# Low parts of the attention values: subtracted by VectorE straight from the bank instead of by GpSimd from a copy

## The chip, the cores and the metric

One core of one Trainium2 chip. The metric is the device time of one execution in microseconds; the times are medians over several executions. Lower is better.

## What is computed

One layer of graph attention with a residual and a layer norm, over 128 graphs of 128 nodes with 512 features, 16 heads of 32, all in float32. The bias is twice the adjacency, since it is given for both encodings.

```python
q, k, v = (split_heads(x @ W.T) for W in (Wq, Wk, Wv))
a = jnp.einsum('bhnd,bhmd->bhnm', q, k) * D ** (-0.5) + (adj + adj)[:, None]
a = jnp.where(jnp.any(a != 0, axis=-1, keepdims=True), a, -jnp.inf)
p = jax.nn.softmax(a, axis=-1)
o = jnp.einsum('bhnm,bhmd->bhnd', p, v).transpose(0, 2, 1, 3).reshape(B, N, D)
return _layernorm(x + o @ Wo.T, axis=-1)
```

## The kernel before

**Precision.** Every product with a weight is split: an operand is a high part (float32 rounded to the form that TensorE takes in one pass, tiles `..._hi`) and a low part (the rest, `..._lo`). `split_product` (L543) makes three matmuls per piece, low x high, high x low, high x high, so 12 matmuls of 512 columns per product. The high part is a copy by ScalarE (ACT), `copy` at L753; the low part is a subtraction, whole minus high: `rest`, on GpSimd at L423 and on VectorE (DVE) at L919.

**Work.** Four graphs form a group (32 groups), four heads a tile (4 tiles per group). One tile of one group is a phase, f = 0 to 127. A phase on each engine:

- TensorE (L699): `scores(f)`, 64 small matmuls into the banks `ps_s`; then, in odd phases from 3 on, `values` of the two phases f-3 and f-2, each into a bank of its own; then four products by a fixed table (`PLAN`, L40): k and q of the next tile, one v, one output product o.
- DVE (L1081): `bias(f)`, 16 instructions of neg_a = -(scores + bias) with the row's minimum, `smallest` (a reduction over all of neg_a), `reciprocals`, `largest`, `stats` and `means` for the layer norm of a graph, `row_factors`, `normalise` and `turn_blocks` (32x32 transposes) for images 0 and 1, then the last four again for images 2 and 3.
- ACT (L876): `exps(f, i)` for images 0 to 3, each four exponentials that wait for that image's bias; after image 0 and after image 1, in odd phases, `values_hi` of the two values; between them `take`, the copies of products out of their banks; `chunk_hi`, the high parts of the inputs; and `normalise`, a row of the layer norm.
- GpSimd (L526): `add` (residual), `chunk_lo` (low parts of the inputs), `values_lo`, `ln` (nine tiny steps of a layer norm). It waits and works in exactly this order.
- SyncE: the DMAs. The transposed blocks leave through `save_blocks` (L336) for a buffer in HBM and come back turned through `move_blocks` (L346) into `e_t`, from which `values` reads. `values(f)` therefore comes two or three phases after the blocks of f.

**Values.** What `values` leaves in its bank is the input of the output products, and so it too has to be split. ACT makes `o_hi` from the bank, then, when GpSimd's subtraction before is over, a second, whole copy `o_sb` from the same bank; GpSimd subtracts `o_hi` from `o_sb` into `o_lo`. These are the lines of ACT (L846 to L851):

```python
copy(o_hi[:, o_slot(g, t), :], values_bank(f)[:, :]).then_inc(o_hi_done, 1)
if f < LAST - 1:
    if f:
        act.wait_ge(o_lo_done, f)
    act.wait_ge(o_hi_done, f + 1)
    copy(o_sb[:, :], values_bank(f)[:, :]).then_inc(values_copied, 1)
```

The four banks `ps_w` are handed round in the order of use (`bank_uses`, L90; `wait_bank`, L561): who wants one waits until its last user's content has been copied, for values until `values_copied`. The values of the last two phases are split by DVE already (`values_lo`, L932, and `values_lo_half`, L938).

Of the kernel before, what the change touches and what calls it, by code (L numbers as in the profile page):

```python
# [11 lines left out]
P = 128  # L12
# [6 lines left out]
TILES = CH  # L19
# [36 lines left out]
LAST = PHASES - 1  # L56
# [26 lines left out]
def valued(f):  # L83

    if f >= LAST - 1:
        return [f - 2]
    return [f - 3, f - 2] if f % 2 and f > 2 else []
# [13 lines left out]
def o_slot(g, tile):  # L101
    return tile + 2 * (g % PAIR) if tile < 2 else tile + 2
# [22 lines left out]
def build(nc, xt_d, x_d, adj_d, wq_d, wk_d, wv_d, wo_d, out_d, blocks_d):  # L125
    ctx = ExitStack()
    with ctx:
        def sb(name, shape, dt=F32):
            return ctx.enter_context(nc.sbuf_tensor(name, shape, dt))
# [4 lines left out]
        def sem(name):  # L134
            return ctx.enter_context(nc.semaphore(name))
# [13 lines left out]
        e_b = sb("e_b", [P, GG * TH * NODES])  # L149
        e_t = sb("e_t", [P, PAIR, GG * TH * NODES])  # L150
        y_sb = sb("y_sb", [P, 512])
        o_sb = sb("o_sb", [P, 512])
        o_hi = sb("o_hi", [P, TILES + 2, 512], F32R)
        o_lo = sb("o_lo", [P, TILES + 2, 512], F32R)
        ident = sb("ident", [P, P])
# [55 lines left out]
        v_copied = sem("v_copied")  # L211
        q_copied = sem("q_copied")
        k_copied = sem("k_copied")
# [16 lines left out]
        r_done = sem("r_done")  # L230
        normalised = sem("normalised")
        o_copied = sem("o_copied")
        values_copied = sem("values_copied")
        opened = sem("opened")
        preloaded = sem("preloaded")
        last_ve_done = sem("last_ve_done")
# [3 lines left out]
        last_lo_done = sem("last_lo_done")  # L240
        o_hi_done = sem("o_hi_done")
        o_lo_done = sem("o_lo_done")
# [26 lines left out]
        def values_bank(f):  # L269
            return ps_w[USE["values", f, 0] % BANKS]  # L270
# [138 lines left out]
        def _(pool):  # L409
# [13 lines left out]
            def rest(out, whole, hi):  # L423
                return pool.tensor_tensor(out, whole, hi.bitcast(F32), ALU.subtract)  # L424
# [7 lines left out]
            def add(f, s):  # L432

                todo = slots(f)
                if todo[s][0] == "o":
                    _, g, i = todo[s]
                    row = x_row(g, i)
                    if GG * g + i >= AHEAD_O:
                        pool.wait_ge(ahead_loaded, 16 * (LATE_O - AHEAD_O))
                    else:  # L440
                        pool.wait_ge(x_loaded[i], 16 * (g + 1))
                    pool.wait_ge(o_copied, count("o", g, i))
                    pool.tensor_tensor(row, y_sb[:, :], row, ALU.add).then_inc(added, 1)  # L443

            def values_lo(f):
                pool.wait_ge(values_copied, f + 1)
                rest(o_lo[:, o_slot(f // TILES, f % TILES), :], o_sb[:, :], o_hi[:, o_slot(f // TILES, f % TILES), :]
                     ).then_inc(o_lo_done, 1)

            def ln(f):  # L450

                n, i = f - O_LAG, (f - O_LAG - 1) % GG
                if n < 1:
                    return
                ve, minus_mean, y, vy, vyy, half, left = (ln_tmp[:, c:c + 1] for c in range(7))

                def own(c):
                    pool.wait_ge(pool_step, 8 * (n - 1) + c)

                if n > 1:  # L460
                    pool.wait_ge(rstd_done, n - 1)
                pool.wait_ge(mean_done, n)
                pool.tensor_tensor(ve, mean_var[:, i, 1:2], eps, ALU.add).then_inc(pool_step, 1)  # L463
                pool.tensor_tensor(minus_mean, mean_var[:, i, 0:1], minus_one, ALU.mult).then_inc(pool_step, 1)
                own(1)
                pool.tensor_tensor(y, ve, minus_half, ALU.pow).then_inc(pool_step, 1)
                own(3)
                pool.tensor_tensor(vy, ve, y, ALU.mult).then_inc(pool_step, 1)
                own(4)
                pool.tensor_tensor(vyy, vy, y, ALU.mult).then_inc(pool_step, 1)  # L470
                own(5)
                pool.tensor_tensor(half, vyy, minus_half, ALU.mult).then_inc(pool_step, 1)
                own(6)
                pool.tensor_tensor(left, half, one_and_half, ALU.add).then_inc(pool_step, 1)
                own(7)
                pool.tensor_tensor(rstd[:, i:i + 1], y, left, ALU.mult).then_inc(pool_step, 1)
                own(8)
                pool.tensor_tensor(shift[:, i:i + 1], minus_mean, rstd[:, i:i + 1], ALU.mult).then_inc(rstd_done, 1)
# [47 lines left out]
            for f in range(PHASES):  # L526
                if f:
                    add(f - 1, -1)
                chunk_lo(window_chunk(f))
                for p in valued(f):  # L530
                    values_lo(p)
                ln(f)
                chunk_lo(late_chunk(f))
                for s in range(len(slots(f)) - 1):
                    add(f, s)
# [6 lines left out]
        def _(pe):  # L542
# [18 lines left out]
            def wait_bank(u):  # L561

                if u >= BANKS:
                    kind, g, index = USES[u - BANKS]
                    free = {"k": k_copied, "q": q_copied, "v": v_copied, "o": o_copied, "values": values_copied}[kind]
                    n = g + 1 if kind == "values" else count(kind, g, index)
                    pe.wait_ge(free, n)

# [183 lines left out]
        def _(act):  # L752
            def copy(out, in_, scale=1.0):  # L753
                return act.activation(out, in_, ACT.Copy, scale=scale)  # L754
# [84 lines left out]
            def values_hi(f):  # L839
                g, t = f // TILES, f % TILES  # L840
                if t > 1 and g:
                    act.wait_ge(made["o"], GG * g)
                elif g > 1:
                    act.wait_ge(made["o"], GG * (g - 1))
                act.wait_ge(values_done, f + 1)
                copy(o_hi[:, o_slot(g, t), :], values_bank(f)[:, :]).then_inc(o_hi_done, 1)  # L846
                if f < LAST - 1:
                    if f:
                        act.wait_ge(o_lo_done, f)
                    act.wait_ge(o_hi_done, f + 1)  # L850
                    copy(o_sb[:, :], values_bank(f)[:, :]).then_inc(values_copied, 1)  # L851

            def values_hi_half(half):
                cols = slice(2 * P * half, 2 * P * (half + 1))
# [63 lines left out]
        def _(dve):  # L918
            def rest(out, whole, hi):  # L919
                return dve.tensor_tensor(out, whole, hi.bitcast(F32), ALU.subtract)  # L920
# [11 lines left out]
            def values_lo(f):  # L932

                slot = o_slot(f // TILES, f % TILES)
                dve.wait_ge(o_hi_done, f + 1)
                rest(o_lo[:, slot, :], values_bank(f)[:, :], o_hi[:, slot, :]).then_inc(last_lo_done, 1)

            def values_lo_half(half):  # L938
                cols = slice(2 * P * half, 2 * P * (half + 1))
# [59 lines left out]
            def bias(f):  # L999
                g = f // TILES  # L1000
                dve.wait_ge(scores_done, f + 1)
                dve.wait_ge(adj_done, g + 1)
                if f:
                    dve.wait_ge(exp_done, GG * f)
                    dve.wait_ge(abs_done, f)
                for i in range(GG):
                    for h in range(TH):
                        last = dve.tensor_tensor_reduce(  # L1008
                            out=neg_a[:, i, h, :], in0=ps_s[h][:, i * NODES:(i + 1) * NODES],
                            in1=adj_sb[:, g % PAIR, i, :], scale=-1.0, scalar=INF, op0=ALU.add, op1=ALU.min,  # L1010
                            accum_out=neg_max[:, i, h:h + 1])
                    last.then_inc(biased, 1)

            def smallest(f):
                dve.wait_ge(biased, GG * (f + 1))
                dve.tensor_reduce(neg_min[:, :].rearrange("p a b -> p (a b)"),  # L1016
                                  neg_a[:, :].rearrange("p a b c -> p (a b) c"), AX.X, ALU.max).then_inc(min_done, 1)
# [62 lines left out]
            dve.wait_ge(xt0_lo_done, CH)  # L1080
            for f in range(PHASES):  # L1081
                bias(f)
                smallest(f)
                reciprocals(f, 0)
                largest(f)
                if f < LAST:
                    stats(f - O_LAG - 1)
                any_nonzero(f)
                if f < LAST:
                    means(f - O_LAG - 1)  # L1090
                row_factors(f, 0)
                if f % TILES == TILES - 1 and f < LAST:
                    double_adj(f // TILES + 1)
                normalise(f, 0)
                if f < LAST:
                    turn_blocks(f, 0)
                else:
                    stats(f - O_LAG - 1)
                    means(f - O_LAG - 1)
                reciprocals(f, 1)  # L1100
                row_factors(f, 1)
                normalise(f, 1)
                if f < LAST:
                    turn_blocks(f, 1)
# [47 lines left out]
```

## Time and profile before

| | us |
|---|---|
| median of 3 runs (lowest to highest) | 1718.62 (1718.35 to 1719.05) |
| the profiled execution's own time | 1717.99 |
| its span, first to last instruction | 1716.2 |
| TensorE busy | 1698.0 (99%) |
| DVE busy | 1633.8 (95%) |
| ACT busy | 1368.4 (80%) |
| GpSimd busy | 962.2 (56%) |
| TensorE's granted clock, mean | 0.999 |

Busy time is the union of an engine's instructions. Matmuls overlap, so that a busy TensorE need not be at its peak. An instruction's duration on DVE and ACT is longer than the distance to the next one where both follow without a wait; the text says "gives way after" for that distance.

### The profile page before, as it was taken

Reading aid. Unit: us, or ns where it says so; the run is one execution under the profiler, and the core shown is the slowest. Engines: PE = TensorE matmul, PEld = TensorE weight load, DVE = VectorE, ACT = ScalarE, POOL = GpSimd, SP = SyncE. Lnnn points to the kernel's source line nnn. Section 1 sums busy time; section 2 is a strip of 40 time slices with the busy share of each in tenths; the row PEclk is TensorE's granted clock in tenths of the full one; section 3 lists DMA queues with packets and bytes.
Section 4 is the critical chain, followed back from the end, with each engine's and each line's share of the span. In section 5 each row is a group of like instructions: output and inputs, shape, how many; then the busy total and the mean of one; then the engine's idle time right before and its main releaser. Section 6 shows DMA issues by size and latency. Waiting matters only on the chain. (4 is left out here: it accounts for less than half of the span.)

```text
span 1716.2 us, 45980 instructions
## 1 busy us (share of the span) xinstructions
PE 1698.0 (99%) x14385; PEld 1383.8 (81%) x14385; DVE 1633.8 (95%) x5814; ACT 1368.4 (80%) x5135; POOL 962.2 (56%) x1512
## 2 busy tenths in 40 slices
PE   8999999999999999999999999999999999999998
PEld 7778888888888888888888888888888888888876
DVE  7999999999999999999999999999999999999997
ACT  7788788778877887788778878887888788778876
POOL 2346556565565565555655655556556556565554
PEclk9999999999999999999999999999999999999999
DMA  7677777777877777777777787777877777777775
GB/s 224 192 203 232 226 227 236 218 215 235 234 221 225 215 232 226 222 224 237 218 226 224 222 236 214 230 233 223 230 213 228 230 220 231 231 217 231 225 227 164
DMA packets 278068, 382.61 MB, mean 223 GB/s; under 512 B 25152, under 2 KB 159552, under 8 KB 277696
## 3 DMA queue, kind: packets, MB, share of 16 engines
q1 hardware_dynamic: 276768, 379.16, 75.3%
q8 instruction: 113, 1.85, 0.5%
q14 instruction: 131, 1.07, 0.2%
q10 hardware_dynamic: 1056, 0.52, 0.1%
HBM read 212.86 MB, written 166.72 MB: 221 GB/s over the span
## 5 line engine op out<-in xcount | busy, mean ns | idle before, releaser
L828 ACT ACTIVATE e_sb<-neg_a,neg_max 128x128 f32<-128x128 f32 x2048 | 793.1, 391 | 185.5 <-DVE neg_max L1008 185.5
L1008 DVE CUSTOM_DVE_ANT_0 neg_a<-ps_s,adj_sb 128x128 f32<-128x128 f32 x2048 | 440.2, 285 | 11.0 <-PE ps_s L634 9.4
L555 PE MATMUL ps_w<-xt_hi,w_lo 128*128 128x512 f32 x1020 | 412.8, 405 | 0.0
L556 PE MATMUL ps_w<-xt_lo,w_hi 128*128 128x512 f32 x1020 | 399.6, 392 | 0.0
L828 ACT ACTIVATION_READ_ACCUMULATOR e_sb<-neg_a,neg_max 128x1 f32 x2048 | 388.9, 190 | 0.0
L1064 DVE STREAM_TRANSPOSE e_b<-e_sb 128x1024 f32<-128x1024 f32 x254 | 316.3, 1245 | 27.3 <-DVE e_sb L1054 0.9
L1054 DVE SCALAR_TENSOR_TENSOR e_sb<-e_sb,r_inv 128x1024 f32<-128x1024 f32 x256 | 318.5, 1244 | 7.9 <-DVE r_inv L1048 0.2
L1016 DVE TENSOR_REDUCE neg_min<-neg_a 128x16 f32<-128x2048 f32 x128 | 292.7, 2286 | 4.4
L424 POOL TENSOR_TENSOR o_lo<-o_sb,o_hi 128x512 fp32r<-128x512 f32 x126 | 163.5, 1298 | 213.8 <-ACT o_sb L754 213.8
L558 PE MATMUL ps_w<-xt_hi,w_hi 128*128 128x512 f32 x1020 | 273.3, 390 | 0.0
L555 PEld LDWEIGHTS ps_w<-xt_hi,w_lo 128*128 128x128 f32 x1020 | 191.5, 188 | 57.5 <-issue 12.7
L558 PEld LDWEIGHTS ps_w<-xt_hi,w_hi 128*128 128x128 f32 x1020 | 191.6, 188 | 40.9
L463 POOL TENSOR_TENSOR ln_tmp<-mean_var,constants 128x1 f32<-128x1 f32 x122 | 31.8, 261 | 343.3 <-DVE mean_var L971 343.3
L556 PEld LDWEIGHTS ps_w<-xt_lo,w_hi 128*128 128x128 f32 x1020 | 191.7, 188 | 37.0
L556 PE MATMUL ps_w<-w_lo,xt_hi 128*128 128x512 f32 x512 | 199.3, 389 | 0.0
L443 POOL TENSOR_TENSOR x_sb<-y_sb,x_sb 128x512 f32<-128x512 f32 x121 | 155.3, 1283 | 78.5 <-ACT y_sb L754 78.5
L555 PE MATMUL ps_w<-w_hi,xt_lo 128*128 128x512 f32 x512 | 199.2, 389 | 0.0
L555 PE MATMUL ps_w<-w_hi,o_lo 128*128 128x512 f32 x496 | 193.2, 390 | 1.7 <-POOL o_lo L424 1.7
L556 PE MATMUL ps_w<-w_lo,o_hi 128*128 128x512 f32 x496 | 193.1, 389 | 0.0
L754 ACT ACTIVATE y_sb<-ps_w 128x512 f32<-128x512 f32 x124 | 74.0, 597 | 129.9 <-PE ps_w L558 129.7
L1008 DVE DVE_READ_ACCUMULATOR2_ANT neg_max<- 128x1 f32 x2048 | 170.8, 83 | 0.0
L634 PEld LDWEIGHTS ps_s<-k_sb,q_sb 32*128 32x128 f32 x4096 | 126.0, 186 | 49.6 <-issue 49.6
(125 smaller groups left out, 2795.7 us busy)
## 6 DMA issues: line engine op xcount, KB each, us to landing
blocks<-e_b SPq DMA_DIRECT2D x1016, 128.0 KB, 2.2
e_t<-blocks SPq DMA_DIRECT2D x126, 1024.0 KB, 7.3
x_sb<-x SPq DMA_DIRECT2D x121, 256.0 KB, 4.9
out<-x_sb SPq DMA_DIRECT2D x121, 256.0 KB, 3.4
xt_raw<-xt SPq DMA_DIRECT2D x120, 256.0 KB, 4.9
adj_sb<-adj SPq DMA_DIRECT2D x32, 256.0 KB, 5.2
neg_a<-xt SPq DMA_DIRECT2D x4, 256.0 KB, 5.7
v_sb<-wv SPq DMA_DIRECT2D x4, 256.0 KB, 7.7
```

What stands on the lines that cost most here:

```text
L424: return pool.tensor_tensor(out, whole, hi.bitcast(F32), ALU.subtract)
L443: pool.tensor_tensor(row, y_sb[:, :], row, ALU.add).then_inc(added, 1)
L555: pe.matmul(out, lhs_lo(c), rhs_hi(c), start=(c == 0), stop=False)
L556: pe.matmul(out, lhs_hi(c), rhs_lo(c), start=False, stop=False)
L558: last = pe.matmul(out, lhs_hi(c), rhs_hi(c), start=False, stop=(c == chunks - 1))
L634: last = pe.matmul(ps_s[h][:, nodes], q_sb[rows, slot, nodes], k_sb[rows, slot, nodes], start=True, stop=True)
L754: return act.activation(out, in_, ACT.Copy, scale=scale)
L828: last = act.activation(e_sb[:, i, h, :], neg_a[:, i, h, :], ACT.Exp, scale=-1.0, bias=neg_max[:, i, h:h + 1], accum_out=sums[:, i, h:h + 1])
L1008: last = dve.tensor_tensor_reduce(out=neg_a[:, i, h, :], in0=ps_s[h][:, i * NODES:(i + 1) * NODES], in1=adj_sb[:, g % PAIR, i, :], scale=- ...
L1016: dve.tensor_reduce(neg_min[:, :].rearrange("p a b -> p (a b)"), neg_a[:, :].rearrange("p a b c -> p (a b) c"), AX.X, ALU.max).then_inc(mi ...
L1054: dve.scalar_tensor_tensor(out=e_sb[:, two].rearrange("p i h n -> p (i h) n"), in0=e_sb[:, two].rearrange("p i h n -> p (i h) n"), scalar=BIG,
L1064: dve.transpose(blocks[:, half], e_sb[:, 2 * half:2 * half + 2].rearrange("p i h (b j) -> p (i h) b j", b=BLOCKS)).then_inc(transposed, 1)
```

## The change

In `values_hi` the second copy goes, with its two waits; `o_sb` and the semaphore `values_copied` go; GpSimd's `values_lo` goes. DVE runs its own `values_lo`, which subtracts `o_hi` from the bank itself, for every phase, between `bias(f)` and `smallest(f)`. The bank of a value is free when that subtraction is over (`o_lo_done`).

```diff
@@ gpsimd
-            def values_lo(f):
-                pool.wait_ge(values_copied, f + 1)
-                rest(o_lo[:, o_slot(f // TILES, f % TILES), :], o_sb[:, :], o_hi[:, o_slot(f // TILES, f % TILES), :]
-                     ).then_inc(o_lo_done, 1)
...
                 chunk_lo(window_chunk(f))
-                for p in valued(f):
-                    values_lo(p)
                 ln(f)
@@ tensor, wait_bank
-                    free = {"k": k_copied, "q": q_copied, "v": v_copied, "o": o_copied, "values": values_copied}[kind]
+                    free = {"k": k_copied, "q": q_copied, "v": v_copied, "o": o_copied, "values": o_lo_done}[kind]
@@ scalar, values_hi
                 copy(o_hi[:, o_slot(g, t), :], values_bank(f)[:, :]).then_inc(o_hi_done, 1)
-                if f < LAST - 1:
-                    if f:
-                        act.wait_ge(o_lo_done, f)
-                    act.wait_ge(o_hi_done, f + 1)
-                    copy(o_sb[:, :], values_bank(f)[:, :]).then_inc(values_copied, 1)
@@ vector, values_lo
                 dve.wait_ge(o_hi_done, f + 1)
-                rest(o_lo[:, slot, :], values_bank(f)[:, :], o_hi[:, slot, :]).then_inc(last_lo_done, 1)
+                rest(o_lo[:, slot, :], values_bank(f)[:, :], o_hi[:, slot, :]
+                     ).then_inc(o_lo_done if f < LAST - 1 else last_lo_done, 1)
@@ vector, the loop over phases
                 bias(f)
+                for p in valued(f):
+                    values_lo(p)
                 smallest(f)
```

DVE, odd phase 5, from the end of its bias on. `ISA ... 128x128` is a bias instruction, `neg_max 128x1` the row minimum that goes with it; after the change the line numbers are those of the changed kernel. Before:

```order
L1008 ISA neg_a,neg_max<-ps_s,adj_sb 128x128
L1008 ISA neg_max 128x1
L1016 TENSOR_REDUCE neg_min<-neg_a 128x16 [waits biased]
L1039 RECIPROCAL recip<-sums 128x8 [waits exp_done,r_done]
L1023 SCALAR_TENSOR_TENSOR abs_max<-neg_max,neg_min 128x16 [waits min_done,nonzero_done]
L1031 TENSOR_SCALAR nonzero<-abs_max 128x16 [waits abs_done,r_done]
L1048 SCALAR_TENSOR_TENSOR r_inv<-recip,nonzero 128x8 [waits nonzero_done,recip_done,normalised]
```


Now:

```order
L995 ISA neg_a,neg_max<-ps_s,adj_sb 128x128
L995 ISA neg_max 128x1
L906 TENSOR_TENSOR o_lo<-ps_w,o_hi 128x512 [waits o_hi_done] x2
L1003 TENSOR_REDUCE neg_min<-neg_a 128x16 [waits biased]
L1026 RECIPROCAL recip<-sums 128x8 [waits exp_done,r_done]
L1010 SCALAR_TENSOR_TENSOR abs_max<-neg_max,neg_min 128x16 [waits min_done,nonzero_done]
L1018 TENSOR_SCALAR nonzero<-abs_max 128x16 [waits abs_done,r_done]
L1035 SCALAR_TENSOR_TENSOR r_inv<-recip,nonzero 128x8 [waits nonzero_done,recip_done,normalised]
```


Two subtractions, each waiting for its high part, stand ahead of the minimum and of all that follows in the phase.

ACT, the odd phase from its first exponential on (`x3` is three more of the four). Before:

```order
L828 ACTIVATE e_sb,sums<-neg_a,neg_max 128x128 [waits biased,transposed]
L828 ACTIVATE e_sb,sums<-neg_a,neg_max 128x128 x3
L754 ACTIVATE o_hi<-ps_w 128x512 [waits values_done,o_made]
L754 ACTIVATE o_sb<-ps_w 128x512 [waits o_hi_done,o_lo_done]
L828 ACTIVATE e_sb,sums<-neg_a,neg_max 128x128 [waits biased]
L828 ACTIVATE e_sb,sums<-neg_a,neg_max 128x128 x3
L754 ACTIVATE o_hi<-ps_w 128x512 [waits values_done,o_made]
L754 ACTIVATE o_sb<-ps_w 128x512 [waits o_hi_done,o_lo_done]
L754 ACTIVATE k_sb<-ps_w 128x512 [waits k_made]
```


Now:

```order
L819 ACTIVATE e_sb,sums<-neg_a,neg_max 128x128 [waits biased,transposed]
L819 ACTIVATE e_sb,sums<-neg_a,neg_max 128x128 x3
L745 ACTIVATE o_hi<-ps_w 128x512 [waits values_done,o_made]
L819 ACTIVATE e_sb,sums<-neg_a,neg_max 128x128 [waits biased]
L819 ACTIVATE e_sb,sums<-neg_a,neg_max 128x128 x3
L745 ACTIVATE o_hi<-ps_w 128x512 [waits values_done,o_made]
L745 ACTIVATE k_sb<-ps_w 128x512 [waits k_made]
```


Between the two high parts only the exponentials of image 1 are left.

## Rows read from the trace of the kernel before

**Rows 1.** The page's first part: busy time and share of each engine.

```profile
PE 1698.0 (99%) x14385; PEld 1383.8 (81%) x14385; DVE 1633.8 (95%) x5814; ACT 1368.4 (80%) x5135; POOL 962.2 (56%) x1512
```

**Rows 2.** Who waited for whom, whole span: total us, times, longest.

```profile
DVE neg_a L1008 <- PE ps_s L634: 9.4, 26, 1.4
...
PE ps_w L658 <- DMA e_t<-blocks: 0.4, 1, 0.4
```

**Rows 3.** Timeline of TensorE, 800 to 831 us: start, duration, instruction.

```profile
804.47 1.17 PE L634 MATMUL ps_s<-k_sb,q_sb 32*128 32x128 f32 x32
...
817.78 1.95 PE L658 MATMUL ps_w<-e_t,v_sb 128*32 128x128 f32 x64
...
825.28 0.39 PE L555 MATMUL ps_w<-w_hi,xt_lo 128*128 128x512 f32 x1
...
830.81 0.39 PE L634 MATMUL ps_s<-k_sb,q_sb 32*128 32x128 f32 x4
```

**Rows 4.** Timeline of DVE, 805 to 833 us; idle time before it in brackets.

```profile
805.71 0.29 DVE L1008 CUSTOM_DVE_ANT_0 neg_a<-ps_s,adj_sb 128x128 f32<-128x128 f32 x1
...
812.61 0.17 DVE L1048 SCALAR_TENSOR_TENSOR r_inv<-recip,nonzero 128x8 f32<-128x8 f32 x1
812.81 1.23 DVE L1054 SCALAR_TENSOR_TENSOR e_sb<-e_sb,r_inv 128x1024 f32<-128x1024 f32 x1
...
817.11 1.25 DVE L1064 STREAM_TRANSPOSE e_b<-e_sb 128x1024 f32<-128x1024 f32 x1
818.28 0.25 DVE L1008 CUSTOM_DVE_ANT_0 neg_a<-ps_s,adj_sb 128x128 f32<-128x128 f32 x1
...
821.75 2.29 DVE L1016 TENSOR_REDUCE neg_min<-neg_a 128x16 f32<-128x2048 f32 x1
...
825.15 1.06 DVE L1048 SCALAR_TENSOR_TENSOR r_inv<-recip,nonzero 128x8 f32<-128x8 f32 x1
826.24 1.23 DVE L1054 SCALAR_TENSOR_TENSOR e_sb<-e_sb,r_inv 128x1024 f32<-128x1024 f32 x1
...
830.54 1.25 DVE L1064 STREAM_TRANSPOSE e_b<-e_sb 128x1024 f32<-128x1024 f32 x1
832.05 0.29 DVE L1008 CUSTOM_DVE_ANT_0 neg_a<-ps_s,adj_sb 128x128 f32<-128x128 f32 x1 [0.26 <-PE ps_s L634]
```

**Rows 5.** Timeline of DVE, the end of the next odd phase.

```profile
857.09 1.25 DVE L1064 STREAM_TRANSPOSE e_b<-e_sb 128x1024 f32<-128x1024 f32 x1
858.39 0.29 DVE L1008 CUSTOM_DVE_ANT_0 neg_a<-ps_s,adj_sb 128x128 f32<-128x128 f32 x1
```

**Rows 6.** Timeline of DVE, first bias of phase 3 and of phase 127.

```profile
55.35 0.25 DVE L1008 CUSTOM_DVE_ANT_0 neg_a<-ps_s,adj_sb 128x128 f32<-128x128 f32 x1
...
1689.76 0.29 DVE L1008 CUSTOM_DVE_ANT_0 neg_a<-ps_s,adj_sb 128x128 f32<-128x128 f32 x1 [1.07 <-PE ps_s L634]
```

**Rows 7.** Timeline of GpSimd, 814 to 828 us.

```profile
816.01 1.04 POOL L478 TENSOR_TENSOR shift<-ln_tmp,rstd 128x1 f32<-128x1 f32 x1
...
824.89 1.29 POOL L424 TENSOR_TENSOR o_lo<-o_sb,o_hi 128x512 fp32r<-128x512 f32 x1 [1.41 <-ACT o_sb L754]
```

**Rows 8.** Timeline of ACT, 819 to 826 us.

```profile
819.28 0.40 ACT L828 ACTIVATE e_sb<-neg_a,neg_max 128x128 f32<-128x128 f32 x1 [1.38 <-DVE neg_max L1008]
...
820.84 0.57 ACT L754 ACTIVATE o_hi<-ps_w 128x512 fp32r<-128x512 f32 x1
...
824.71 0.59 ACT L754 ACTIVATE k_sb<-ps_w 128x512 f32<-128x512 f32 x1
825.18 0.40 ACT L828 ACTIVATE e_sb<-neg_a,neg_max 128x128 f32<-128x128 f32 x1
```

**Rows 9.** Timeline of DVE, the two subtractions at the kernel's end.

```profile
1701.31 0.69 DVE L920 TENSOR_TENSOR o_lo<-ps_w,o_hi 128x512 fp32r<-128x512 f32 x1 [0.27 <-ACT o_hi L754]
1701.92 0.41 DVE L920 TENSOR_TENSOR o_lo<-ps_s,o_hi 128x256 fp32r<-128x256 f32 x1
```

**Rows 10.** Transfers into e_t issued between 834 and 900 us.

```profile
DMA to landing us min/median/max: 6.9/7.0/8.4
```

More of the change, by code:

```diff
@@ L151, in build @@
         y_sb = sb("y_sb", [P, 512])
-        o_sb = sb("o_sb", [P, 512])
         o_hi = sb("o_hi", [P, TILES + 2, 512], F32R)
@@ L232, in build @@
         o_copied = sem("o_copied")
-        values_copied = sem("values_copied")
         opened = sem("opened")
```

## The prediction

> **What bounds the kernel now.** I read the page's busy times first. TensorE is busy 99% of the span, VectorE (DVE) 95%, ScalarE (ACT) 80%, GpSimd (POOL) 56% [rows 1]. Two engines stand near full, so the next view is who waits for whom. DVE waits for scores only 26 times, 9.4 us in all, and TensorE waits for the transposed blocks once [rows 2]. Neither engine waits for the other to speak of: two chains have almost the same length.
>
> The timelines show which is longer. From scores to scores over two phases, TensorE takes 830.81 - 804.47 = 26.34 us [rows 3], and it has matmuls all the way. DVE's biases have the same distance, 832.05 - 805.71 = 26.34, and in it DVE stands still once: its last transpose starts at 830.54, such a transpose gives way to the next instruction after 1.17 us (817.11 to 818.28), so it could go on at 831.71, and it starts at 832.05, released by TensorE: 0.34 us free in this pair [rows 4]. In the next pair, which also doubles the adjacency, 857.09 + 1.17 = 858.26 against 858.39: 0.13 us free [rows 5]. **So TensorE sets the pace, with DVE 0.47 us in 52.68 behind it** (805.71 to 858.39, four phases). The whole loop confirms the group: from the bias of phase 3 to that of phase 127 it is 1689.76 - 55.35 = 1634.4 us [rows 6], 31 groups of 52.7.
>
> **The change, part by part.** Phases are numbered f = 0 to 127; in every odd f from 3 to 125 the values of two earlier phases are handled, 62 times.
>
> *GpSimd's 126 subtractions go.* They are on GpSimd, which has time. But one of them touches DVE. In an even phase the row factors at 812.61 give way to the next instruction after 0.20 us; in the odd phase the same instruction, at 825.15, lasts 1.06 and gives way after 1.09 [rows 4]. It ends at 826.21, and GpSimd's second subtraction, started at 824.89, ends at 826.18 [rows 7]: DVE was held until GpSimd had finished. With that subtraction gone I take back 0.89 us per odd phase. Bounds: 0, if something else of GpSimd's stands there then, and 1.09. I take 0.89, because in even phases, where GpSimd has only its small layer norm steps at this place, the row is short.
>
> *ACT's 126 second copies go.* ACT has time; what counts is that its second high part comes earlier. After the first exponential of an odd phase at 819.28, four of them take 1.56 us (to the first high part at 820.84), a copy gives way after 0.47 (824.71 to 825.18) and ends after 0.57 [rows 8]. Without the copy into o_sb the second high part ends at 819.28 + 1.56 + 0.47 + 1.56 + 0.57 = 823.44.
>
> *DVE gets 126 subtractions, two in a row between its bias and its minimum in odd phases.* The nearest row is the same subtraction, from the bank, at the kernel's end: 0.69 us long, and the next starts 0.61 after it [rows 9]. The first needs the high part that ended at 820.84 + 0.57 = 821.41, and starts at once when the bias is through, about 821.7. The second has to wait for the high part of 823.44; with a handover of some 0.06 it starts at 823.50, and the minimum follows at 824.11 where it started at 821.75 [rows 4]. **That is +2.36 us per odd phase: 1.22 of work and 1.14 of waiting for ACT.** Behind the waiting instruction stands all of DVE's phase: minimum, factors, both normalisations, both transposes and the next bias; ACT's exponentials of images 2 and 3 do not hang on it. Bounds: 1.22, if the high part came in time, and 2.6, if ACT starts a little late too. I take the timeline's 2.36.
>
> The Trainium skill, page "VectorE: DVE Perf Modes", section "The DRAIN you can't avoid", says that the next operation does not start until the pipeline has emptied. By that each subtraction would cost its full length, 0.69 where the rows show the next one 0.61 behind, and the sum would come out about 10 us higher; the trace decides, and I keep 0.61.
>
> *The bank is given back by DVE, not by ACT's copy.* The v and o products of the same phase, behind k and q, reuse these two banks. The first subtraction is over at about 822.4 and the second at 824.2, and the v product began at 825.28, the o product after it [rows 3]: no cost. The tile o_lo is complete at about 824.2 instead of 826.2, so the output products have it earlier. The buffer and two waits of ACT (for the old subtraction, and for its own first copy) go for nothing.
>
> *What is late next.* When DVE is the slower one, TensorE runs ahead until it meets the transposed blocks, which hang on DVE's transposes over two DMA hops. Their last hop lands 7.0 us after issue in the median, and TensorE waits for it only once in the profile [rows 2, 10]. So TensorE will stand at the values in odd phases by about what DVE lost, at most some 2 us. That costs nothing: values that start even 0.5 us after the bias has begun take 1.95 us [rows 3] and are done before ACT turns to the first high part, 2.6 us after that beginning (818.28 to 820.84). GpSimd's adding of the inputs comes earlier relative to DVE, but it stands behind the layer norm chain in GpSimd's own order, whose last step at 816.01 is held by DVE's second normalisation [rows 7]; so it cannot fall on that one.
>
> **The sum.** Four phases: 52.68, minus the free 0.34 and 0.13, minus 2 x 0.89, plus 2 x 2.36, is 55.15 us of DVE work without a gap, longer than TensorE's 52.68. That is +2.47 per group, times 31: +76.6. Phase 126 handles one value, +0.61 more. The last phase has another 0.61 ahead of its minimum, and there ACT's exponentials start earlier by the copy that is gone: I set it at nothing. Together +77 us. The profiled execution had a span of 1716.2 and took 1717.99, 0.6 below the median of the three runs; so 1718.6 + 77 = 1796 us. The three runs lie within 0.7 us, and about 0.2% (3.4 us) is what a measurement of this kernel can tell from no change.
>
> **Rivals.**
>
> *A: TensorE stays the bound, not slower.* The time freed on DVE (0.89 per odd phase and the 0.47 of gaps) pays for the subtractions. That decides the other way if 4 subtractions plus their waits cost no more than 52.68 - 50.43 = 2.25 us per group, 0.56 each with no wait. The rows speak against both: 0.61, and the second high part 1.1 us late. With slots of 0.61 and no wait it would be 50.43 + 2.44 = 52.87, +6 us, 1725; with slightly shorter slots 1718.6. For it: TensorE's higher busy share. Chance 0.05.
>
> The Trainium skill, page "Perfetto Trace Analysis", section "Identifying the Most-Contended Engine", takes the engine with the highest share as the one to optimise (and itself warns that matmul busy time misleads). By that rule TensorE stays the bound as long as DVE's busy time, 1634 + 77 - 55, is below 1698 [rows 1], and the time stays at 1718.6. It is this rival's case, and I give it no more than its 0.05, since an engine that works in order pays for its waits as well.
>
> *B: the held instruction stays held.* Something else of GpSimd's, an addition or a chunk subtraction shifted by the new lag, falls on a DVE instruction that it can hold. Price 0.89 per odd phase, 62 times: +55, 1851 us. For it: the 1.09 shows such holds are real. Against: in GpSimd's order nothing but the layer norm steps is left between the chunk's subtraction and the next addition. Chance 0.08.
>
> *C: the wait for the second high part is smaller or larger than I read*, by half: 62 x 0.57 = 35 us either way, 1761 or 1831. Against: every piece of that chain is a row. Chance 0.10.
>
> *D: TensorE loses speed when it stands still for a while*, or the blocks come so late that both engines wait in turn. One more us per pair would be 1858. Chance 0.03.
>
> **How the numbers follow.** The forecast has the remaining 0.74. Its own spread is 0.2 us per odd phase, 12 us, so 1784 to 1808; taking in part of C on both sides the range is 1776 to 1822. Faster needs something that no row shows: 0.01. Within 0.2% needs rival A with shorter slots: 0.03. Slower by over 0.2%: 0.96.
>
> **What would show it.** In the new profile DVE is busy about 1634 + 77 - 55 = 1656 us of 1793 and TensorE still 1698; DVE has some 62 waits of about 1.1 us at the subtraction, released by ACT's o_hi, about 70 us in all; 126 subtractions of 0.69; no wait of DVE for scores in the loop; the row factors near 0.17 us in odd phases too; pairs of phases at about 27.5 us, odd ones near 14.9 and even ones still 12.57; TensorE with idle time at the values or in front of them, some 1.2 us per pair. It would be wrong if the odd phase of DVE is not longer by about 1.5 us net, if the subtraction does not wait for ACT, or if DVE still waits for scores.

## The result, and the profile after

| | before | after |
|---|---|---|
| median, us | 1718.84 | 1794.97 |
| lowest to highest, us | 1718.35 to 1719.58 | 1793.28 to 1795.61 |
| ratio, 95% interval | | 1.0441 (1.0429 to 1.0454) |
| profiled execution, its span, us | 1716.2 | 1792.7 |
| DVE busy, us | 1633.8 | 1652.2 |
| TensorE busy, us | 1698.0 | 1713.5 |

The change makes the kernel 76 us slower. Forecast were 77. The page's first part after, against [rows 1]:

```profile
PE 1713.5 (96%) x14385; PEld 1388.1 (77%) x14385; DVE 1652.2 (92%) x5940; ACT 1289.2 (72%) x5009; POOL 797.3 (44%) x1386
```

Every engine has a lower share than before, also the one that now sets the pace. DVE is busy for only 18 us more: 87 us of subtractions, less 48 us at the row factors, whose instructions sum up to 46 us against 94, less some 17 us in which neighbours overlap and which the union counts once, and a few us of small differences. The kernel lost 76. The rest must be standing still. Who waited for whom (total us, times, longest), against [rows 2]:

```profile
ACT e_sb L819 <- DVE neg_max L995: 401.7, 126, 6.7
...
DVE o_lo L906 <- ACT o_hi L745: 72.0, 64, 1.2
PEld ps_w L649 <- issue: 63.0, 51, 3.9
...
PE ps_w L649 <- DMA e_t<-blocks: 50.7, 42, 3.7
...
DVE neg_a L995 <- PE ps_s L625: 2.7, 3, 1.3
```

DVE has a new wait of 72.0 us for ACT's high part, and nearly none for scores. TensorE waits for the transposed blocks at the values. `issue` marks time for which the profile shows nothing that was waited for. DVE in an odd phase (start, duration, instruction, idle time before it in brackets), to be laid beside [rows 4]:

```profile
857.39 0.25 DVE L995 CUSTOM_DVE_ANT_0 neg_a<-ps_s,adj_sb 128x128 f32<-128x128 f32 x1
...
860.74 0.69 DVE L906 TENSOR_TENSOR o_lo<-ps_w,o_hi 128x512 fp32r<-128x512 f32 x1
862.58 0.69 DVE L906 TENSOR_TENSOR o_lo<-ps_w,o_hi 128x512 fp32r<-128x512 f32 x1 [1.15 <-ACT o_hi L745]
863.18 2.28 DVE L1003 TENSOR_REDUCE neg_min<-neg_a 128x16 f32<-128x2048 f32 x1
...
866.92 0.17 DVE L1035 SCALAR_TENSOR_TENSOR r_inv<-recip,nonzero 128x8 f32<-128x8 f32 x1
867.12 1.23 DVE L1041 SCALAR_TENSOR_TENSOR e_sb<-e_sb,r_inv 128x1024 f32<-128x1024 f32 x1
...
872.60 0.25 DVE L995 CUSTOM_DVE_ANT_0 neg_a<-ps_s,adj_sb 128x128 f32<-128x128 f32 x1
...
885.14 0.25 DVE L995 CUSTOM_DVE_ANT_0 neg_a<-ps_s,adj_sb 128x128 f32<-128x128 f32 x1
```

The minimum starts 5.79 us after the first bias instruction where it started at 3.47: +2.32. The row factors last 0.17, not 1.06. The even phase, 872.60 to 885.14, is 12.54 long against 12.57. And ACT beside it, against [rows 8]:

```profile
858.38 0.40 ACT L819 ACTIVATE e_sb<-neg_a,neg_max 128x128 f32<-128x128 f32 x1 [3.12 <-DVE neg_max L995]
...
859.95 0.58 ACT L745 ACTIVATE o_hi<-ps_w 128x512 fp32r<-128x512 f32 x1
860.42 0.39 ACT L819 ACTIVATE e_sb<-neg_a,neg_max 128x128 f32<-128x128 f32 x1
...
861.96 0.58 ACT L745 ACTIVATE o_hi<-ps_w 128x512 fp32r<-128x512 f32 x1
```

The second high part ends at 862.54, DVE's second subtraction starts at 862.58. Ahead of it on ACT stand the four exponentials of image 1: DVE waits for work that ACT does first only because it comes first in its order. The first bias of phase 3 and of phase 127, against [rows 6]:

```profile
54.01 0.25 DVE L995 CUSTOM_DVE_ANT_0 neg_a<-ps_s,adj_sb 128x128 f32<-128x128 f32 x1
...
1766.70 0.25 DVE L995 CUSTOM_DVE_ANT_0 neg_a<-ps_s,adj_sb 128x128 f32<-128x128 f32 x1
```

The loop is 1712.7 us long, 78.3 more than before, or 55.25 per group of four phases. The start is 1.3 us shorter and the end, 26.0 us, 0.4 shorter.

### The profile page after: what moved, and what is told of

Same layout as the page of the kernel before. It is cut to its first block and busy times, and to the rows that moved or that the text cites. A ratio compares the mean times of both kernels' runs of the same rounds, so it can differ in the third digit from the quotient of the medians.

```text
span 1792.7 us, 45729 instructions
## 1 busy us (share of the span) xinstructions
PE 1713.5 (96%) x14385; PEld 1388.1 (77%) x14385; DVE 1652.2 (92%) x5940; ACT 1289.2 (72%) x5009; POOL 797.3 (44%) x1386
## 3 DMA queue, kind: packets, MB, share of 16 engines
q14 instruction: 129, 1.06, 0.2%
## 5 line engine op out<-in xcount | busy, mean ns | idle before, releaser
L649 PE MATMUL ps_w<-e_t,v_sb 128*32 128x128 f32 x4064 | 138.3, 280 | 50.9 <-DMA e_t<-blocks 50.7
L422 POOL TENSOR_TENSOR xt_lo<-xt_raw,xt_hi 128x512 fp32r<-128x512 f32 x120 | 154.5, 1288 | 26.7 <-ACT xt_hi L745 26.7
L625 PE MATMUL ps_s<-k_sb,q_sb 32*128 32x128 f32 x4096 | 150.3, 283 | 16.5 <-issue 15.8
```

Of the source, the lines that this page charges most:

```text
L625: last = pe.matmul(ps_s[h][:, nodes], q_sb[rows, slot, nodes], k_sb[rows, slot, nodes], start=True, stop=True)
L649: last = pe.matmul(out[HD * h:HD * (h + 1), i * P:(i + 1) * P], v_sb[:, g % PAIR, i, cols], weights, start=True, stop=True)
```

## The experiments

Each is timed beside the kernel before on the same chip; what is called "after" is the changed kernel at 1794.97.

### The wait: both subtractions behind the minimum

In the changed kernel:

```diff
                 bias(f)
+                smallest(f)
                 for p in valued(f):
                     values_lo(p)
-                smallest(f)
```

> The changed kernel with both subtractions moved behind the minimum (smallest, then values_lo twice). Theory (ACT's second high part, ready 5.2 us after the first bias instruction, is what DVE waited for): the minimum covers that time, the 62 waits of 1.12 us go, four phases of DVE come to 55.00 - 2 x 1.12 = 52.76 us, just above TensorE's 52.68, so about 1721 us (1718 to 1726). Rival (the subtractions themselves or the bank handed back later cost the 76 us, the wait is only where it shows): near 1795 us still.

Measured: 1721.47 us, ratio to before 1.0018 (1.0009 to 1.0028). The same instructions stand on DVE, in another order, and 73.5 of the 76 us are gone. DVE in an odd phase:

```profile
824.86 2.29 DVE L1003 TENSOR_REDUCE neg_min<-neg_a 128x16 f32<-128x2048 f32 x1
827.06 1.28 DVE L906 TENSOR_TENSOR o_lo<-ps_w,o_hi 128x512 fp32r<-128x512 f32 x2
828.26 0.20 DVE L1026 RECIPROCAL recip<-sums 128x8 f32<-128x8 f32 x1
```

The two subtractions run without a gap, 1.20 us for both (827.06 to 828.26). Removing a wait of 1.12 us in 62 phases explains 70 us. Of the 3.5 that are left, 2.3 can be a hold in one phase of after (phase 43, below) that this kernel does not have, and late blocks are a candidate for the rest; they are not accounted for one by one. That the time stops at 1721 and doesn't fall by more is TensorE's pace again: bias to bias over two phases is 26.36 us in the median of the run, against 26.34 in [rows 3, 4].

### The wait made longer: ACT's second copy back

In the changed kernel ACT copies again after each high part, from a weight tile into a tile that nobody reads:

```diff
                 copy(o_hi[:, o_slot(g, t), :], values_bank(f)[:, :]).then_inc(o_hi_done, 1)
+                if f < LAST - 1:
+                    if f:
+                        act.wait_ge(scratched, f)
+                    act.wait_ge(o_hi_done, f + 1)
+                    copy(o_sb[:, :], w_hi[:, WEIGHT["k"], 0, :].bitcast(F32)).then_inc(scratched, 1)
```

> The changed kernel, where ACT again makes a second copy of 512 columns after each high part (into a buffer nobody reads, from a weight tile, so that the bank is left alone). Theory: the second high part comes 0.69 us later (5.26 instead of 4.57 us after the first bias instruction, as in the kernel before), DVE's wait grows by that in each of 62 odd phases, +43 us, 1838 us. Rival (DVE waits for the values or the blocks behind the high part, ACT has room): 1795 us.

Measured: 1838.21 us, +43.2 over after, ratio to before 1.0697 (1.0681 to 1.0713). DVE's wait is the row that grew, from 72.0 to

```profile
DVE o_lo L913 <- ACT o_hi L747: 117.0, 63, 2.1
```

45 us more of waiting, 43 us more of time, 0.70 per odd phase: the copy that stands ahead of the second high part counts at full price, though ACT had been busy only 72% of the span in after.

### One more subtraction, ahead of the wait and behind it

```diff
                 for n, p in enumerate(valued(f)):
+                    if f < LAST - 1 and n == 0:      # n == 1 in dup_behind
+                        again(p)                     # the same subtraction, into an unused tile
                     values_lo(p)
```

> The changed kernel with one more DVE subtraction of the same kind and bank (into a buffer nobody reads) ahead of the wait for the second high part. Theory: 0.61 us of work inside a wait of 1.12 us, nothing changes: 1795 us, the wait down to 0.5 us. Rival (DVE's cost is its instructions wherever they stand): 62 x 0.61 = +38 us, 1833 us.

> The same additional subtraction, but behind the wait for the second high part. Theory: DVE is the bound and nothing covers it: 62 x 0.61 = +38 us, 1833 us. By a full pipeline drain behind each instruction (0.69 us) +43 us, 1838 us. Rival (TensorE or the blocks set the pace): less than 10 us more.

Measured: 1791.53 us ahead of the wait, 3.4 less than after; 1831.69 behind it, +36.7. The 3.4 us lie in two phases: in after, phase 15 lasts 16.44 us and phase 43 lasts 17.38 (what happened in them is told below), and here both last 15.06. DVE's wait in the first:

```profile
DVE o_lo L908 <- ACT o_hi L747: 35.0, 64, 0.6
```

and in the second, where the additional subtraction is the one that waits:

```profile
DVE o_sb L908 <- ACT o_hi L747: 75.4, 62, 1.2
```

The same instruction costs nothing or 0.59 us, by its place alone. The 0.59 is the distance between two subtractions in [rows 9] (0.61), not their duration of 0.69.

### What GpSimd holds on DVE

Two kernels, built from the changed one, give GpSimd work again in odd phases, on operands nobody else uses: one at the places that the high parts set, one that begins when DVE has finished `largest`.

```diff
                 chunk_lo(window_chunk(f))
+                if f % 2 and 2 < f < LAST - 1:
+                    for n in range(2):               # once in pool_abs
+                        idle_lo(f, n)                # waits for o_hi_done; for abs_done in pool_abs
                 ln(f)
```

> The changed kernel with two GpSimd subtractions of 512 columns per odd phase again (operands and target that nobody else uses), each started by the high part of a value: one stands beside the bias and DVE's first subtraction, the other beside DVE's second subtraction and the minimum. Theory: DVE's instruction with one operand in a bank, and the minimum with a single operand, are not held; row factors come later (9.2 us), when GpSimd is through: 1795 us. Rival (any GpSimd subtraction holds DVE): +0.5 to +1.3 us per odd phase, 1826 to 1875 us.

> The changed kernel with one such GpSimd subtraction per odd phase, started when DVE has finished largest (8.35 us after the first bias instruction), so that it is under way when the row factors (two operands in SBUF) begin at 9.18 us. Theory: they are held until it ends at about 9.7 us, they give way at about 9.77 instead of 9.38, 62 x 0.39 = +24 us, 1819 us. Rival (the long row factors of the kernel before had another cause): 1795 us.

Measured: pool_hi 1793.37 us, as after. pool_abs 1837.82, +42.9 instead of the +24 expected. In pool_hi GpSimd and DVE side by side, GpSimd first:

```profile
858.74 1.28 POOL L424 TENSOR_TENSOR o_sb<-w_hi 128x512 f32<-128x512 f32 x1 [1.97 <-ACT o_hi L756]
860.76 1.29 POOL L424 TENSOR_TENSOR o_sb<-w_hi 128x512 f32<-128x512 f32 x1 [0.74 <-ACT o_hi L756]
```

```profile
858.89 0.69 DVE L917 TENSOR_TENSOR o_lo<-ps_w,o_hi 128x512 fp32r<-128x512 f32 x1
860.71 0.69 DVE L917 TENSOR_TENSOR o_lo<-ps_w,o_hi 128x512 fp32r<-128x512 f32 x1 [1.14 <-ACT o_hi L756]
861.32 2.28 DVE L1014 TENSOR_REDUCE neg_min<-neg_a 128x16 f32<-128x2048 f32 x1
```

DVE's subtraction at 858.89 starts inside GpSimd's and keeps its 0.69; so does the minimum at 861.32. In pool_abs:

```profile
914.56 1.30 POOL L424 TENSOR_TENSOR o_sb<-w_hi 128x512 f32<-128x512 f32 x1 [5.93 <-DVE abs_max L1021]
```

```profile
915.02 0.87 DVE L1029 TENSOR_SCALAR nonzero<-abs_max 128x16 f32<-128x16 f32 x1
915.80 0.17 DVE L969 BATCH_NORM_AGGREGATE mean_var<-ln_stats 128x2 f32<-128x6 f32 x1
916.02 0.17 DVE L1046 SCALAR_TENSOR_TENSOR r_inv<-recip,nonzero 128x8 f32<-128x8 f32 x1
```

Held was not the row factors but `nonzero` ahead of them, which has one operand in SBUF: 0.87 us instead of 0.16, until GpSimd ended at 915.86. 0.70 times 62 is 43 us, what was measured. My expectation had the mechanism and named the wrong instruction. The Trainium skill, page "SBUF — State Buffer", section "Who interferes with whom", names both kinds that can be held: an instruction with two SBUF inputs, and a `tensor_scalar` in its fast mode. The rows agree, and also with its remark that a reduction isn't held; whether `nonzero` ran in that mode, no row shows.

### Half of the change: only the first value

The kernel before, with DVE subtracting the first value of an odd phase from its bank and GpSimd the second one from the copy; the semaphores that follow from it are left out here.

```diff
@@ scalar, values_hi
-                if f < LAST - 1:
+                if f < LAST - 1 and f % 2:
@@ gpsimd, the loop
                 for p in valued(f):
-                    values_lo(p)
+                    if p % 2 and p < LAST - 1:
+                        values_lo(p)
@@ vector, the loop
                 bias(f)
+                for p in valued(f):
+                    if p % 2 == 0:
+                        values_lo(p)
                 smallest(f)
```

> The kernel before, but only the first of the two values of an odd phase is subtracted by DVE from its bank; the second goes through ACT's copy and GpSimd as before. Theory: 0.61 us more on DVE per odd phase with no wait, and GpSimd's subtraction now from 5.9 to 7.2 us, over before the row factors at 7.5 us, so no hold of 0.89: four phases of DVE 52.23 - 1.78 + 1.22 = 51.67 us, under TensorE's 52.68: 1715 to 1719 us, not above the kernel before. Rival (the row factors are still held): 52.23 + 1.22 = 53.45 us of DVE, +24 us, 1743 us.

Measured: 1723.08 us, ratio 1.0029 (1.0018 to 1.0040), neither number: slower than before by 4 to 5 us. The trace has the reason. GpSimd, then DVE:

```profile
828.68 1.29 POOL L425 TENSOR_TENSOR o_lo<-o_sb,o_hi 128x512 fp32r<-128x512 f32 x1 [4.66 <-ACT o_sb L760]
```

```profile
829.09 0.91 DVE L1030 SCALAR_TENSOR_TENSOR abs_max<-neg_max,neg_min 128x16 f32<-128x16 f32 x1
...
830.81 0.17 DVE L1055 SCALAR_TENSOR_TENSOR r_inv<-recip,nonzero 128x8 f32<-128x8 f32 x1
```

The row factors are free as expected, but GpSimd's subtraction, now earlier, holds `largest` for 0.73. The hold had moved to another small instruction. So the next run puts `stats`, 0.6 us of one operand, over the end of GpSimd's subtraction:

```diff
                 smallest(f)
+                if f < LAST:
+                    stats(f - O_LAG - 1)
                 reciprocals(f, 0)
                 largest(f)
-                if f < LAST:
-                    stats(f - O_LAG - 1)
```

> The run hybrid, with stats (one operand) moved in front of reciprocals and largest. In hybrid the instruction largest, of two operands, lasted 0.91 instead of 0.18 us, held by GpSimd's subtraction from 5.92 to 7.21 us. Theory (this hold is what put hybrid 4 to 5 us over the kernel before): stats covers it, largest begins at about 7.1 us and is held by 0.1 at most, four phases of DVE come to 51.8 us, under TensorE's 52.68: 1716 to 1720 us. Rival (another cause, such as the banks or the copies): 1723 us as in hybrid.

Measured: 1718.60 us, ratio 0.9999 (0.9990 to 1.0008). `largest` is down to 0.39:

```profile
825.61 0.39 DVE L1030 SCALAR_TENSOR_TENSOR abs_max<-neg_max,neg_min 128x16 f32<-128x16 f32 x1
```

That is TensorE's pace once more, level with the kernel before and no better.

### What the hold was worth before

The hold of 0.89 us stands in my sum as a credit. Taken away alone, by shortening GpSimd's second subtraction in the kernel before to 16 of its 512 columns:

```diff
-                rest(o_lo[:, o_slot(f // TILES, f % TILES), :], o_sb[:, :], o_hi[:, o_slot(f // TILES, f % TILES), :]
-                     ).then_inc(o_lo_done, 1)
+                cols = slice(0, 512 if f % 2 == 0 else 16)
+                rest(o_lo[:, o_slot(f // TILES, f % TILES), cols], o_sb[:, cols],
+                     o_hi[:, o_slot(f // TILES, f % TILES), cols]).then_inc(o_lo_done, 1)
```

> The kernel before, but GpSimd's subtraction for the second value of an odd phase covers 16 of 512 columns (the low parts of the other 496 columns of these values are left out, as zeros set at the start). Theory: the 0.89 us in which DVE's row factors were held lay under TensorE's pace; they go from the trace, DVE waits for scores instead (0.9 us more per odd phase, some 60 us in all against 9), and the time stays at 1718 (1716 to 1720). Rival (the hold was on the path, TensorE's 26.34 us per pair of phases followed DVE): 55 us faster, 1664 us, or a good part of it.

Measured: 1715.62 us, ratio 0.9982 (0.9973 to 0.9991). The row factors' instructions sum up to 43.6 us here against 94.3 before, so some 51 us of holding are gone, and only 3 of them were on the path. The rest turned into waits of DVE, 28 us more for ACT's exponentials and 20 more for scores:

```profile
DVE recip L1044 <- ACT e_sb L833: 30.2, 62, 1.7
DVE neg_a L1013 <- PE ps_s L639: 29.0, 57, 1.2
```

against 2.0 us for the exponentials and 9.4 for scores in the kernel before.

### The adjacency off DVE: inconclusive

```diff
@@ vector, on top of late
-                if f % TILES == TILES - 1 and f < LAST:
-                    double_adj(f // TILES + 1)
@@ scalar
                 chunk_hi(late_chunk(f))
+                if f % TILES == TILES - 1 and f < LAST:
+                    double_adj(f // TILES + 1)
```

> The run late, and ACT doubles the adjacency instead of DVE (0.33 us per four phases off DVE). Theory: 52.76 - 0.33 = 52.43 us of DVE, under TensorE's 52.68: the pace is TensorE's again, 1718 to 1721 us, at or just under late. Rival (late is slowed by a wait and not by the sum of DVE's work): the same time as late.

Measured: 1720.98 us, ratio 1.0018 (1.0009 to 1.0027): within the expected numbers of both. The pairs of phases are TensorE's 26.34 us in the median, and the loop is as long as in `late` (1637.4 against 1637.6 us) though DVE is busy for 5 us less (1638.3 against 1643.5), which speaks for TensorE's pace in both; the time alone doesn't tell it from `late`. The loop of both is still 3 us longer than before (1634.4), which is not traced. Some more lies outside the steady loop, where DVE now gives the low parts later and TensorE waits for them: in both for 2 us at 1699, and in late_adj for 2.6 near 88 us.

```profile
PE ps_w L546 <- DVE o_lo L913: 3.1, 3, 2.6
...
PE ps_w L679 <- DVE o_lo L913: 1.9, 1, 1.9
```

## Why the prediction was right, step by step

**Two chains of nearly equal length, TensorE's just ahead.** Right, and the ground of everything else: late, hybrid_stats and short_second all come back to 26.34 to 26.36 us per pair, whatever they do to DVE, and in after every addition to DVE that no wait covers shows in the time.

**+2.36 per odd phase: 1.22 of work and 1.14 of waiting.** Measured +2.32, with 1.15 idle before the second subtraction in the phase shown and 72.0 us over the 64 times. Each half was shown by itself: the work by dup_behind (0.59 per subtraction against 0.61), the waiting by late (away) and copy_kept (longer).

**-0.89 for the held row factors.** The mechanism is right, the sum over the run was a little too large. After, the first row factors of an odd phase last 0.17 us in all of the 62 phases. Before, they were held in 57 of them, mostly to 1.05, and in five not at all: 0.97 in the mean, so that the credit was 50 us and not 55. That GpSimd's subtraction had held them was a reading of two ends 0.03 us apart; pool_abs shows the mechanism with a subtraction made for the purpose, on another instruction. Leaving the subtraction out was also not the only thing that freed them: they came 2.3 us later, and pool_hi, with both subtractions back on GpSimd, is as fast as after.

**The sum.** 55.15 us per group against 55.25 measured, +77 us against +76. The agreement to 1 us is better than its parts, and in so far luck. The loop was 1.1 us longer than I had it (78.3 against 77.2), and the start and the end, which I had set at nothing, gave 1.3 and 0.4 back. Inside the loop the credit was 5 us too large, and phases 15 and 43 cost 1.4 and 2.3 us that no term stands for; 2.32 in place of 2.36 and even phases 0.03 us shorter took back a part of that, and what took back the rest is not traced.

**TensorE stands at the values by some 2 us at most, at no cost.** The place was right, the size was too small: it waited up to 3.7 us for the blocks, and from phase 7 on its scores began as much as 4.2 us ahead of DVE's bias in odd phases. Mostly it cost nothing. In phase 15 (219.83 to 236.28, 16.4 us instead of 15.1) TensorE stood 3.66 us for the blocks, the scores of the next phase followed late, and DVE waited 1.31 us for them. TensorE, then DVE:

```profile
221.46 1.93 PE L649 MATMUL ps_w<-e_t,v_sb 128*32 128x128 f32 x32 [3.66 <-DMA e_t<-blocks]
```

```profile
236.28 0.29 DVE L995 CUSTOM_DVE_ANT_0 neg_a<-ps_s,adj_sb 128x128 f32<-128x128 f32 x1 [1.31 <-PE ps_s L625]
```

That is the second half of rival D, in single phases. Its first half, that TensorE loses speed when it stands still, is in the trace too: after stands of 4.10, 3.66, 2.44 and 2.99 us its granted clock went down to 0.5 (1.2 instead of 2.4 GHz) for some 3.4 us each, from 77.9, 221.2, 415.8 and 634.2 on, where the loop before has no such stretch. A stand of 2.60 us, up to 332.0, left it at 1.0. The second of these stretches lies in phase 15 and has its part in that phase's 1.4 us; how much is not told apart from the blocks. TensorE's busy time, forecast as still 1698 us, came to 1713.5, 13 us of the difference at the values.

**GpSimd's addition "cannot fall on" the second normalisation.** That step failed, in one phase of the steady loop, phase 43. (Row factors also lasted 0.7 to 1.2 us in three of the first phases; two of these the kernel before has as well.) The rows of DVE there:

```profile
620.11 1.14 DVE L1035 SCALAR_TENSOR_TENSOR r_inv<-recip,nonzero 128x8 f32<-128x8 f32 x1
621.29 2.27 DVE L1041 SCALAR_TENSOR_TENSOR e_sb<-e_sb,r_inv 128x1024 f32<-128x1024 f32 x1
```

and of GpSimd:

```profile
619.80 0.19 POOL L471 TENSOR_TENSOR shift<-ln_tmp,rstd 128x1 f32<-128x1 f32 x1
619.94 1.29 POOL L441 TENSOR_TENSOR x_sb<-y_sb,x_sb 128x512 f32<-128x512 f32 x1
621.19 1.29 POOL L422 TENSOR_TENSOR xt_lo<-xt_raw,xt_hi 128x512 fp32r<-128x512 f32 x1
```

I had taken it that the last layer norm step is always held by DVE's normalisation, since it was in the phase I looked at. Here it was through before (0.19 us instead of 1.04), the addition came at once and held DVE's row factors, and the chunk's subtraction held the normalisation: 2.3 us in this phase. That is rival B; hybrid showed it in every odd phase.

**Rival A and the rule of the highest share.** Refuted. TensorE's matmul share is the highest after as before, 96% against DVE's 92%, and DVE sets the pace: dup_behind adds 0.59 us of DVE work per odd phase and the time follows. The Trainium skill's page "Perfetto Trace Analysis", section "Identifying the Most-Contended Engine", takes the engine of the highest share, and my reading of it was too short: it judges TensorE's headroom by its LDWEIGHTS share (and by its arithmetic rate) and not by matmul busy time. The weight loads' share (PEld) is 77% after and 81% before, both under DVE's 92 and 95%. By matmul share the rule names TensorE in both kernels, by weight loads DVE in both; the runs show TensorE's pace before (short_second) and DVE's after (dup_behind). Neither share tells two engines apart that are this close. Busy shares leave out what an engine waits for in its own order.

**The drain behind each instruction** (0.69 and not 0.61 per subtraction) would have made dup_behind 43 us slower; it was 36.7. The Trainium skill's page "VectorE: DVE Perf Modes", section "The DRAIN you can't avoid", leaves room for this, which I had passed over: it adds that a next operation that is not held starts earlier.

## What to carry to other kernels

Where an engine works in order and is near the bound, ask of every added instruction when its operand is ready, before asking how long it takes: the same subtraction cost nothing in front of a wait and its full 0.6 us behind it, and moving two of them by one instruction took back 73 of 76 us. An offload that looks idle on a third engine can hold small instructions on DVE; when anything moves, look which instruction now starts inside the other engine's, since the hold moves along. And a wait or hold that is seen on an engine one step behind the bound is worth little until that engine becomes the bound: 51 us of holding were worth 3.

## What the runs showed of the hardware that I had not expected

A GpSimd subtraction of 512 columns (1.29 us) holds a DVE `tensor_scalar` with one SBUF operand of 16 columns (0.87 instead of 0.16 us) as it does instructions with two, but not a subtraction with one operand in a bank (0.69), nor a reduction (2.28), each started inside it. The kernel before has such holds already: two of its 32 doublings of the adjacency (a `tensor_scalar` of 512 columns, 0.42 us) last 1.52 and 1.54, each started inside a GpSimd instruction of 512 columns. The subtraction of 512 columns lasts 0.69 us on DVE whether its first operand lies in a bank or, as for the weights at the start, in SBUF.
